# Running sums as one fp32 product instead of a high and a low part, a three-table routing of the first token blocks, and new slots for all side work

## The reference, cut to what matters

```
x = x + 0.5 * L0_ffn(layernorm(x))      # pass 0: top-2 of 8 experts, hidden 256
x = x + L0_attn(layernorm(x))           # gated attention: square(relu(q k^T / n)) v
x = x + 0.5 * L0_ffn(layernorm(x))      # pass 1
x = x + 0.5 * L1_ffn(layernorm(x))      # pass 2: top-2 of 8 experts, hidden 352
x = x + L1_attn(layernorm(x))           # linear attention, 16 heads
x = x + 0.5 * L1_ffn(layernorm(x))      # pass 3
```

```
kv  = cumsum(einsum('bhtf,bhtg->bhtfg', K, V), axis=2)      # 16 heads x 4 x 8 = 512 columns a token
Z   = 1 / (einsum('bhtf,bhtf->bht', Q, cumsum(K, axis=2)) + 1e-06)
out = einsum('bhtf,bhtfg->bhtg', Q, kv) * Z[..., None]
```

## Time and profile before

| what | value |
|---|---|
| three runs, median | 777.35 us (775.86, 777.35, 780.17) |
| the profiled execution, its own time | 774.85 us |
| its span, first to last instruction | 773.1 us |
| mean granted TensorE clock | 0.922 of full speed |
| PE busy | 628.1 us, 81% of the span |
| DVE busy | 411.4 us, 53% |
| POOL busy | 318.0 us, 41% |
| ACT busy | 264.8 us, 34% |

### The profile page before, as it was taken

One profiled execution on the slowest core, in us unless ns is written; L12 is line 12 of the kernel. 1 busy time (PEld: TensorE's weight loads), 2 busy tenths in 40 slices (PEclk: granted clock), 3 DMA queues, 4 the chain that ended last, 5 costly groups with the idle time before them and its releaser, 6 DMA issues.

```text
span 773.1 us, 15404 instructions
## 1 busy us (share of the span) xinstructions
PE 628.1 (81%) x4590; PEld 574.4 (74%) x4590; DVE 411.4 (53%) x1385; ACT 264.8 (34%) x549; POOL 318.0 (41%) x352
## 2 busy tenths in 40 slices
PE   2588588959969779677779787998899999977977
PEld 1387577848759569567779786797788987877977
DVE  6743443805517237154434344485985977844446
ACT  2233342523424324223233233433633435323321
POOL 3635344270441622745452516405615546154124
PEclk9999899988979999888989889899997989998999
DMA  7568566634626437575766567464574665647853
GB/s 246 157 218 261 155 179 218 190 99 135 189 61 186 135 103 227 152 215 148 217 201 195 155 170 224 133 182 137 156 204 116 181 190 164 182 136 227 241 144 82
DMA packets 113268, 133.57 MB, mean 173 GB/s; under 512 B 10931, under 2 KB 76227, under 8 KB 112806
## 3 DMA queue, kind: packets, MB, share of 16 engines
q1 hardware_dynamic: 104998, 115.79, 51.6%
q0 software_dynamic: 8192, 16.79, 7.2%
HBM read 103.83 MB, written 28.71 MB: 171 GB/s over the span
## 4 chain that ended last, share of the span: by engine, by line
PE 56%; DVE 15%; another core or an unknown queue 12%; issue 9%; ACT 5%; POOL 2%; DMA 0%; DVEq 0%; ACTq 0%
PE up_gate L1022 15%; PE up_gate L1015 12%; PE y L976 9%; DVE hidden L679 3%; PE side L1037 2%; PE y L978 2%; PE side L1103 2%; PE side L1053 2%; POOL b_rstd L481 2%; DVE x_res L715 1%; ACT hidden L574 1%; DVE rms_out L701 1%; PE side L1111 1%; PE side L1048 1%
## 5 line engine op out<-in xcount | busy, mean ns | idle before, releaser
L679 DVE TENSOR_TENSOR hidden<-up_gate,hidden 128x256 f32<-128x256 f32 (+1 forms) x240 | 115.7, 488 | 265.3 <-ACT hidden L574 94.7
L1022 PE MATMUL up_gate<-rows_T,up 128*128 128x128 f32 x1440 | 198.5, 289 | 30.6 <-issue 12.3
L1022 PEld LDWEIGHTS up_gate<-rows_T,up 128*128 128x128 f32 x1440 | 184.3, 202 | 38.8 <-issue 19.8
L574 ACT ACTIVATE hidden<-up_gate 128x256 f32<-128x256 f32 (+1 forms) x240 | 104.5, 437 | 300.0 <-PE up_gate L1015 103.1
L489 POOL DMA_INDIRECT rows_dram<-rms_out,rows_of x128 | 130.2, 1017 | 173.1 <-DVE rows_of L825 131.0
L1015 PE MATMUL up_gate<-rows_T,up 128*128 128x128 f32 x960 | 139.3, 291 | 20.0 <-ACT rows_T L579 13.6
L507 POOL DMA_INDIRECT y_rows<-y_dram,rows_of x120 | 121.6, 1013 | 71.3 <-issue 35.8
L1015 PEld LDWEIGHTS up_gate<-rows_T,up 128*128 128x128 f32 x960 | 127.0, 203 | 28.9 <-issue 26.8
L481 POOL TENSOR_TENSOR b_rstd<-b_var,minus_half 128x8 f32<-128x8 f32 x16 | 26.8, 1675 | 146.8 <-DVE b_var L696 146.8
L976 PE MATMUL y<-down,hidden 128*128 x480 | 78.1, 287 | 6.9 <-DVE hidden L679 4.9
L976 PE MATMUL y<-down_a,hidden 128*128 x480 | 77.3, 286 | 0.0
(11 more groups left out here) (188 smaller groups left out, 693.0 us busy)
## 6 DMA issues: line engine op xcount, KB each, us to landing
up<-in_up SPq DMA_DIRECT2D x120, 352.0 KB
up<-in_up SPq DMA_DIRECT2D x120, 256.0 KB
rows<-rows_dram SPq DMA_DIRECT2D x47, 256.0 KB
y_dram<-y_tile SPq DMA_DIRECT2D x45, 256.0 KB
rows_dram<-zeros SPq DMA_DIRECT2D x12, 256.0 KB, 3.7
rows<-rows_dram SPq DMA_DIRECT2D x16, 192.0 KB
y_dram<-y_tile SPq DMA_DIRECT2D x15, 192.0 KB
rows_dram<-rms_out,rows_of POOLq DMA_INDIRECT x128
```

What stands on the lines that cost most here:

```text
L574: act.activation(hid[n % 4][:, 0:w], src, ACT.Silu).then_inc(silu_done, 1)
L679: dve.tensor_tensor(h, u, h, ALU.mult).then_inc(mult_done, 1)
L1022: last = pe.matmul(U[q % 3][:, c * P:(c + 1) * P], upW[n % RING][:, at + c * P:at + (c + 1) * P], rows_, start=True, stop=True)
```

## The change

The split into a high and a low part is taken out: kv_hi, kv_lo, tri_r and ones_r go, and TensorE multiplies POOL's products as they are, in fp32, by the fp32 matrices tri and ones. It waits for POOL's kv_ready in place of VectorE's lo_ready. Every number of the slot tables is new, and so are GATHER, LOAD_ROWS, LEAD and the slots of the late matrices. "guess" has a new wait for the skip of the block before. The early store of the last pass moves by two slots.

```diff
-GATHER = 3
+GATHER = 4
 STORE = 3
 DOWN = 2
 ROWS_AT = 2
-LOAD_ROWS = 3
-LEAD = 38
+LOAD_ROWS = 4
+LEAD = 41
...
-ROUTE = (({"stats": 3, "guess": 3, "root": 8, "norm": 8, "skip": 15, "z": 9, "score": 12, "first": 12, "second": 15, "rank": 17, "assign": 17, "weights": 25, "scatter": 23},
+ROUTE = (({"stats": 0, "guess": 10, "root": 10, "norm": 11, "skip": 19, "z": 14, "score": 15, "first": 18, "second": 19, "rank": 26, "assign": 26, "weights": 29, "scatter": 26},
...
-LATE_T, LATE_STORE, LATE_LOAD = (LATE_AT - LATE + at for at in (-8, -7, -6))
-LATE_MATRIX = [LATE_AT - LATE + at for at in (1, 2, 8, 11, 12, 13, 14)]
+LATE_T, LATE_STORE, LATE_LOAD = (LATE_AT - LATE + at for at in (-12, -10, -4))
+LATE_MATRIX = [LATE_AT - LATE + at for at in (0, 0, 1, 3, 4, 13, 15)]
...
-                    if END_ROUND[r] + (STORE if (s, g) != LAST else 1) - 1 == t:
+                    if END_ROUND[r] + (STORE if (s, g) != LAST else 3) - 1 == t:
...
-                    if j in (13, 14, 15, 16):
-                        t = j - 13
-                        act.wait_ge(kv_ready, 4 * ka - 3 + t)
-                        act.activation(kv_hi[t][:, :], R[3 + t], ACT.Copy).then_inc(hi_ready, 1)
...
                 if o == at["guess"]:
+                    after(dve, skip_ready, k - 1)
                     variance(b_st, b_mv, b_ve, 1e-6, True).then_inc(b_var, 1)
...
-                if l == 1 and j in (14, 15, 16, 17):
-                    t = j - 14
-                    dve.wait_ge(hi_ready, 4 * ka - 3 + t)
-                    dve.tensor_tensor(kv_lo[t][:, :], R[3 + t], kv_hi[t][:, :].bitcast(F32), ALU.subtract).then_inc(lo_ready, 1)
...
-                        pe.wait_ge(lo_ready, 4 * ka - 3 + t)
+                        pe.wait_ge(kv_ready, 4 * ka - 3 + t)
...
-                        pe.matmul(o, tri_r[:, :], kv_hi[t][:, :], start=True, stop=False)
-                        last = pe.matmul(o, tri_r[:, :], kv_lo[t][:, :], start=False, stop=(t % 2 == 0))
+                        last = pe.matmul(o, tri[:, :], R[3 + t], start=True, stop=(t % 2 == 0))
                         if t % 2:
-                            pe.matmul(o, ones_r[:, :], kv_hi[t - 1][:, :], start=False, stop=False)
-                            last = pe.matmul(o, ones_r[:, :], kv_lo[t - 1][:, :], start=False, stop=True)
+                            last = pe.matmul(o, ones[:, :], R[2 + t], start=False, stop=True)
```

More of the change, by code:

```diff
@@ L65 @@
 ROWS_AT = 2
-LOAD_ROWS = 3
-LEAD = 38
[L68 to L74, removed]
+LOAD_ROWS = 4
+LEAD = 41
+LAG = (8, 32, 4, 29, 14)
+COMBINE = (((8, 11),),
+           ((17, 17),),
+           ((8, 10),),
+           ((8, 11),))
+ATTENTION = (({3: 11, 4: 13, 5: 13, 6: 14, 7: 16, 8: 17, 9: 18, 10: 18, 11: 18, 12: 19, 13: 19, 14: 20, 15: 21},),
@@ L75 @@
              None,
-             ({3: 13, 4: 14, 5: 15, 6: 16, 7: 17, 8: 18, 9: 18, 10: 18, 11: 19, 12: 19, 13: 22, 14: 22, 15: 23, 16: 24, 17: 26, 18: 27, 19: 27, 20: 29, 21: 30},),
+             ({3: 10, 4: 10, 5: 11, 6: 11, 7: 13, 8: 14, 9: 14, 10: 14, 11: 15, 12: 15, 13: 16, 14: 16, 15: 17, 16: 18, 17: 19, 18: 20, 19: 20, 20: 22, 21: 23},),
              None)
-ROUTE = (({"stats": 3, "guess": 3, "root": 8, "norm": 8, "skip": 15, "z": 9, "score": 12, "first": 12, "second": 15, "rank": 17, "assign": 17, "weights": 25, "scatter": 23},
[L79 to L83, removed]
@@ new lines @@
+ROUTE = (({"stats": 0, "guess": 10, "root": 10, "norm": 11, "skip": 19, "z": 14, "score": 15, "first": 18, "second": 19, "rank": 26, "assign": 26, "weights": 29, "scatter": 26},
+          {"stats": 11, "guess": 11, "root": 11, "norm": 14, "skip": 16, "z": 16, "score": 17, "first": 20, "second": 20, "rank": 22, "assign": 23, "weights": 30, "scatter": 24},
+          {"stats": 5, "guess": 6, "root": 10, "norm": 11, "skip": 23, "z": 14, "score": 16, "first": 16, "second": 17, "rank": 27, "assign": 27, "weights": 28, "scatter": 28},),
+         ({"stats": 21, "guess": 21, "root": 24, "norm": 24, "skip": 25, "z": 26, "score": 27, "first": 27, "second": 28, "rank": 30, "assign": 30, "weights": 40, "scatter": 30},),
+         ({"stats": 18, "guess": 19, "root": 19, "norm": 24, "skip": 31, "z": 26, "score": 27, "first": 27, "second": 27, "rank": 29, "assign": 29, "weights": 36, "scatter": 30},),
+         ({"stats": 24, "guess": 24, "root": 24, "norm": 25, "skip": 30, "z": 26, "score": 27, "first": 27, "second": 28, "rank": 29, "assign": 29, "weights": 31, "scatter": 31},))
@@ L195, in macaron @@
         xT = sb("attn_xT", NT)
-        kv_hi = [sb(f"kv_hi{i}", NT, F32R) for i in range(TB)]
-        kv_lo = [sb(f"kv_lo{i}", NT, F32R) for i in range(TB)]
-        tri_r = sb("tri_r", P, F32R)
-        ones_r = sb("ones_r", P, F32R)
         spare = sb("spare", 2)
@@ L319, in macaron @@
         qkv_ready, min_ready, v_ready, exp_ready = sem("qkv_ready"), sem("min_ready"), sem("v_ready"), sem("exp_ready")
[L320 removed]
+        phi_ready, kv_ready, kcum_ready, den_used = sem("phi_ready"), sem("kv_ready"), sem("kcum_ready"), sem("den_used")
         cum_ready, cum_used = sem("cum_ready"), sem("cum_used")
@@ L657, in _ @@
             act.activation(spare[:, 0:1], ones[:, 0:1], ACT.Silu)
-            act.activation(tri_r[:, :], tri[:, :], ACT.Copy)
-            act.activation(ones_r[:, :], ones[:, :], ACT.Copy).then_inc(const_pe, 1)
             act.wait_ge(norm_loaded, 32)
@@ L1192, in _ @@
             pe.wait_ge(consts, 7)
-            pe.wait_ge(const_pe, 2)
+            pe.wait_ge(const_pe, 1)
             pe.wait_ge(norm_loaded, 32)
```

1 line of the change is left out of this document (removed).

## The result

| | before | after |
|---|---|---|
| median of 4 runs | 778.76 us (775.86 to 781.60) | 796.92 us (791.84 to 799.92) |
| the profiled execution, span | 773.1 us | 793.7 us |
| first up product | 31.6 us | 40.2 us |
| TensorE busy | 628.1 us | 636.5 us |

The ratio is 1.0208 with a 95% interval of 1.0159 to 1.0257: slower by 2.1%, clear of noise, and outside the range of 761 to 790. The forecast, no change, was wrong.

What follows compares the result with a forecast made beforehand. TensorE was taken to set the pace, with VectorE also a bound in part of layer 1's attention and waits setting layer 0's. Terms summed to +0.4 us, a median of 777.8; the forecast was the middle, 776.5, range 761 to 790.

Steps and rivals of the forecast that it cites:

- The running sums: Products of the sums: +8 us for fp32 on TensorE, -4.6 for waits gone, -2 for freed VectorE and ScalarE work.
- The start: Blocks 0 to 2 of pass 0: block 1's root behind four transfers, 8 us later, 4 regained; +4, bounds 0 and +9.
- Block 2 of pass 0: Its period of 44.3 us lengthens because "assign" moves and joins scatter to gather; +4.5 us, bounds 0 and +7.
- Layer 0's steady periods: Other periods of layer 0's attention: stages 9, 10, 11 share a slot within the burst's time; 0, bounds -5 and +6.
- Layer 1's slots: Waits for the norm (3.8 us) and score's copy (2.3 us) go, with slots now between; -6, bounds -6 and 0.
- Between passes 1 and 2: TensorE's waits of 6.4 and 2.8 us mostly go as "z" stands four slots later; -5, bounds -9 and 0.
- The end: Last combine's transfers wait for block 2's combine, whose second half stands a slot later; +1.5 us, bounds 0 and +2.5.
- C: Rival, slower, about 788 us: POOL's joined bursts make TensorE's signals late at layer 1's sums; chance 0.28.
- B: Rival, faster, about 765 us: VectorE bounds layer 1's attention, each of four periods gains 2.5 us more; chance 0.32.
- D: Rival: the sums' added 2.2 us a block fall into TensorE's gaps; 772 us, inside the forecast's range, no separate chance.
- the rule of the Trainium skill: Line 865, two SBUF inputs on VectorE, and GpSimd's SBUF reads exclude each other; removal gives back 3.4 us of VectorE.

Runs made afterwards that it cites:

- plain pair: b_plain and a_plain: the kernels before and after with indirect transfers replaced by plain ones, on one chip; 631.0 and 625.0 us.
- b_plain: Kernel before with the 248 indirect transfers of scatter and gather replaced by plain ones to and from fixed places (computes something else); 631.0 us, 0.7957 of before.
- a_plain: Changed kernel with its indirect transfers replaced by plain ones to and from fixed places (computes something else); 625.0 us, 0.7886 of before.
- after_again: Changed kernel, unchanged, run again beside the kernel before on a chip of 793 us; 1.0170 of before.
- a_start: Changed kernel with LEAD and pass 0's routing slots from the kernel before; 1.0095 of before on the chip of 793 us.
- b_fp32_2: Kernel before with only the running sums as one fp32 product, split removed, every slot as before; 1.0015 of before on a chip of 790 us.
- b_l0_2: Kernel before with layer 0's attention, pass 0's combine and pass 1's routing in the changed kernel's slots; 0.9914 of before on a chip of 790 us.
- a_l1_2: Changed kernel with layer 1's attention, pass 2's combine, pass 3's routing and late matrices in before's slots; 1.0041 of before on a chip of 790 us.
- b_l1: Kernel before with layer 1's attention, pass 2's combine and pass 3's routing in the changed kernel's slots, split kept; 1.0101 of before.
- a_misc: Changed kernel with GATHER and LOAD_ROWS at 3 as before; 1.0060 of before on the chip of 793 us.
- a_split: Changed kernel with the split in two fp32r parts put back, in the new slots; 0.9968 of before on the chip of 645 us.
- b_fp32: Kernel before with only the running sums as one fp32 product, every slot as before; 1.0035 of before on the chip of 645 us.
- a_rows3: Changed kernel with rows transposed three slots ahead of their first tile instead of two, and loaded a slot earlier; 835.2 us on a chip of 791 us.

## Why the prediction was wrong, step by step

The plain pair gives, for each pass, what the indirect transfers cost (period sums with them less without, one execution each; the traces with them are of another chip, so a few us are chip against chip):

| us | start | pass 0 | pass 1 | pass 2 | pass 3 | end | all |
|---|---|---|---|---|---|---|---|
| before less b_plain | -0.7 | 31.4 | 49.8 | 39.8 | 24.2 | -1.7 | 142.8 |
| after less a_plain | 4.1 | 39.3 | 40.9 | 48.3 | 38.0 | -0.5 | 170.1 |
| more in the changed kernel | 4.8 | 7.9 | -8.9 | 8.5 | 13.8 | 1.2 | 27.3 |

The change is worth -6.7 us of span without them (623.6 against 630.3) and costs 27.3 us more with them: +20.6. The loss itself was 13 us on the chip of after_again, which would make this some 20.

The prediction's bounds, added up, reach from 744 to 808 us and not from 750 to 800. So the measured time lies within the bounds of the terms, and the range cut it off.

- **The running sums: right in sum.** Terms +8, -4.6 for their waits and -2 for the freed work, +1.4 in all; measured alone +0.15% (interval -0.25 to +0.54%) and +0.35%. The product's price was met closely: TensorE's busy time rose by 8.4 us. VectorE's fell by 22.7, where I said 14; without indirect transfers it falls by 14.2. In the changed kernel's timeline an odd sum's products start 0.87 apart, and the next tile 0.85 later, where 0.86 was taken:

```profile
496.50 1.02 PE L1124 MATMUL side<-attention,tri 128*128 128x512 f32 x2
497.37 1.02 PE L1126 MATMUL side<-attention,ones 128*128 128x512 f32 x2
498.22 0.94 PE L1009 MATMUL up_gate<-rows_T,up 128*128 128x128 f32 x7
```

- **The start: mechanism right, size a little small.** The root of block 1 comes at 24.62 behind four transfers, as worked out, and the chain ends within a microsecond of the forecast 32.5. The one-hot product took 6.70 us, where I left its 5.25 unchanged, and so the first up product came at 40.2 and not at 39.6:

```profile
24.62 1.70 POOL L477 TENSOR_TENSOR b_rstd<-b_var,minus_half 128x8 f32<-128x8 f32 x1
...
31.84 6.70 PE L1018 MATMUL side<-attention,rms_out 128*128 128x512 f32 x8 [0.44 <-DVE scores L754]
40.23 2.04 PE L1002 MATMUL up_gate<-rows_T,up 128*128 128x128 f32 x16 [1.69 <-issue]
```

  I let 4 of the 8 us come back. The profile has 4.4 left after block 0; a_start puts it at 6.

- **Block 2 of pass 0, +4.5: the number right, the reason not** (44.3 to 50.4 us, +6.1). On the chip of 790 to 793 us it is 43.1 us in b_fp32_2 and 51.8 in after_again. The scatter and the gather did join into one burst (115.6 to 136.1 us). But I put that on "assign", which moves from slot 24 to 30, and a_start and b_l0_2 have it at slot 24: their bursts are joined as well (in b_l0_2 the scatter starts at 102.43, the gather at 112.81), and the period is longer still, 54.7 and 56.6 us. It is layer 0's new slots that make this period long. With the old ones slots 30 and 31 take 3.2 and 5.0 us, and in b_l0_2 1.4 and 1.8, and the gather is ready by the time the scatter ends. The packed stages 9, 10 and 11 stand in slot 33 here: it takes 21.1 us in b_l0_2, 22.2 in a_start and 10.8 in the changed kernel, and 6.8 in a_plain.

- **Layer 0's steady periods, 0: wrong side.** They gave 5.0, 4.7 and 3.1 us. The slots show how: before, slot 49 took 14.3 us, of which b_plain needs 4.8, and slot 48 took 6.2, of which it needs 2.2. The changed kernel puts stages 9, 10 and 11 into slot 48: 6.8 us, with or without late signals, though the burst (167.9 to 188.4 us) begins 1.5 us ahead of it. The hold-up comes in slot 49, now 11.8 us, and slots 45, 46 and 56 are shorter (1.6, 2.7 and 1.8 us in place of 3.3, 3.6 and 2.8). That the packing is cheap there is luck of place as far as the runs tell: in block 2 of b_l0_2, where the burst begins 11.4 us ahead of the packed slot, it is the dearest of all. Without late signals it gains nothing: 38.1 against 37.7 us. With this, the terms of layer 0, +4.5 together, are -7 us by b_l0_2, its long block 2 included.

- **Layer 1's slots, -6: this is the step that failed.** I read the waits for the norm and the score, found slots put between them, and took the 6.1 us off. They did go, and without late signals the new slots are the better ones (120.5 against 134.4 us for the first three periods of pass 3 in the plain pair). But these slots also carry the place of the scatter and of the attention's round trips, and I priced neither. a_l1_2 and b_l1 put them at +10 and +8 us where the forecast had -6; b_l1 is the firmer of the two. In the third period of pass 3, before's two bursts of eight stand apart:

```profile
682.67 1.08 POOL L507 DMA_INDIRECT y_rows<-y_dram,rows_of  x1 [1.38 <-DMA y_dram<-y_tile]
...
697.21 1.02 POOL L489 DMA_INDIRECT rows_dram<-rms_out,rows_of  x1 [4.33 <-DVE rows_of L825]
```

  They cost 49.1 - 40.4 = 8.7 us; the joined one of sixteen costs 50.8 - 32.0 = 18.8, nearly all in slots 213 and 214 (22.2 us against 4.1). In the first period of the changed kernel six scatters stand apart between POOL's products, and only the last two join the gather. There the transfers cost 51.5 - 45.8 = 5.7 us, in slot 187 alone (8.1 against 2.4), where before they cost 51.3 - 46.3 = 5.0. Whether the joining makes the difference, or that one period has sums and the other bare tiles, no run isolates.

- **Between passes 1 and 2, -5: wrong.** The later "z" did remove the wait of 6.4 us. The stall did not go but moved a slot: slots 122 and 123 took 8.0 and 2.5 us before, and slots 123 and 124 take 8.8 and 4.0 now. The first two periods of pass 2 grew from 46.2 and 47.6 us to 49.8 and 52.3, and in place of the 6.4 us up products wait 14.3 us for copies of rows:

```profile
PE up_gate L1009 <- ACT rows_T L575: 6.6, 1, 6.6
```

```profile
PE up_gate L1009 <- ACT rows_T L575: 7.7, 2, 6.8
```

  Putting the old slots back gave 6 us with wide intervals. Some 3 us of the second period are there without late signals too (36.8 us in a_plain, 33.6 in b_plain), in slot 149.

- **GATHER and LOAD_ROWS at 4: no term at all.** I put them at nothing without a reason. a_misc takes them back and is 9 us faster, with the intervals just overlapping.

- **The end, +1.5: not settled.** The stretch behind the last tile grew from 14.7 to 17.8 us. But it is 17.7 us in b_fp32_2 and 14.8 in b_l0_2, both with before's slots there, so the 3.2 us cannot be put down to the change. The early gathers started at 753.60 before, 4.9 us ahead of the last tile's up products at 758.5; now they start 2.8 us ahead of them (775.8). This does not settle it either, for in after_again they start 4.5 us ahead and the stretch is 17.9 us:

```profile
773.05 1.00 POOL L520 DMA_INDIRECT y_rows<-y_early,early_rows_of  x1 [15.59 <-issue]
```

**The rivals.** C, with late signals as its mechanism and joined bursts as its place, was the nearest, at 788 against 796.9. It gave the start 8, block 2 its 7, and layer 1 only 1.5 us a period. It put the loss into every period with running sums. Against the plain pair, a period's late signals cost 5.2 us more than before in the last of pass 2, but 0.7 and 1.0 in the first two of pass 3, 1.9 less in the third of pass 2, and 10.1 more in the third of pass 3, which has no sums. Its own sign, periods over 53 us in pass 3 with waits at the sums, did not come. I held against C that pass 3 has slots enough to lay bursts in; the third period shows that room is no help. B fell for these chips: the first three periods of pass 3 sum to 150.6 us, as before's 152.7. Without late signals they do get much shorter, but by the slots and not by B's freed VectorE: on the chip of 645 us they sum to 123.5 us in a_split, which keeps the split, and to 141.1 in b_fp32, which does not. D differs from the forecast by 4 us in one term. The 1 to 2 us measured for the product alone stand nearer to the forecast's +1.4 than to D's -2.6, but only the sum of the terms was measured.

**On the rule of the Trainium skill** that the prediction weighed (SBUF — State Buffer, "Who interferes with whom"): b_fp32_2 takes line 865 away and gains nothing that can be measured, so the 3.4 us of VectorE that the rule would return are not worth time here. The three long ones of line 865 (1143, 2155 and 2175 ns, at 499.05, 553.31 and 656.21 us) do each overlap a product of POOL's line 540; no run tells whether that is the exclusion.

## What to carry to other kernels

Where one cause holds up an engine at a fixed time (here TensorE's late signals while GpSimd issues indirect transfers), do not price waits one at a time: find what stands under the hold-up. The same three stages packed into one slot cost next to nothing extra where the burst had just begun (slot 48, 6.8 us) and 14 us where it had run for 11 us (slot 33 of b_l0_2, 21.1). When a wait vanishes in an experiment and its time comes up at the next instruction, as in passes 2 and 3 of a_rows3, it was the place and not the cause. And time a schedule on more than one chip: the same tables were 0.997 of before on one and 1.017 on another.

## What the runs showed of the hardware that I had not expected

- **Two kinds of chips.** The kernel before takes 644.9 us on one chip and 779 to 793 us on the others. The difference goes with late signals. On the first, ScalarE has no "remote" wait in any of four profiled kernels, and 129 to 193 us of them in each one profiled on the others with its indirect transfers. On the first, the kernel with the fp32 product has 37.6 us in pass 0's block 3; with the same slots the others have 51 to 52.
- **On a chip that has late signals they went with the indirect transfers; being issued by GpSimd is not enough.** The plain transfers of b_plain go through the same queue with the same load. The queues' row of before and of b_plain:

```profile
q0 software_dynamic: 8192, 16.79, 7.2%
```

```profile
q0 software_dynamic: 8192, 16.79, 8.2%
```

  The Trainium skill (DMA: Bandwidth & Descriptors, "SWDGE vs HWDGE vs iDMA") says that direct and indirect transfers from GpSimd both have their descriptors made in software. The rows agree, and so that path alone does not make signals late. What differs is GpSimd's time: eight plain ones take 4.35 us (545.17, above) and eight indirect ones 10.0 (689.74 to 699.77). The plain ones also go to and from fixed rows that lie together, and these two were not tried apart. Why the indirect ones hold TensorE's signals, on some chips and not on another, stays open.
- **The size of it.** Replacing 248 indirect transfers by plain ones took 161 us off, 20% of the program. The transfers themselves had looked hidden: GpSimd was busy in 41% of the span.
